# First layer's experts with tokens as rows, weighted after the multiplication

## The reference, cut to what matters

```python
gate_probs = softmax(xn @ gate_w.T + gate_b)          # 10 experts, 2 of them null
weights, selected = top_k(gate_probs, 2)              # null experts weigh nothing, the rest is normalised
combine_w = ...                                       # [tokens, 8], at most two entries of a row not zero
expert_out = einsum('td,edh->teh', xn, expert_w) + expert_b
ffn = einsum('te,teh->th', combine_w, expert_out)
x = x + attention(xn) + ffn
```

## Time and profile before

| what | value |
|---|---|
| time, median of three runs | 1821.56 us (1819.24 to 1825.79) |
| the profiled execution's own time | 1823.29 us |
| its span, first to last instruction | 1821.3 us |
| TensorE busy | 1721.1 us, 94% of the span |
| VectorE busy | 1015.6 us, 56% |
| ScalarE busy | 831.5 us, 46% |
| GpSimd busy | 385.6 us, 21% |
| mean granted TensorE clock | 0.958 |
| steps of `layer0_mix` | about 48 to 427 us of the span |

### The profile page before, as it was taken

How to read it: one execution, slowest core, us unless ns; L and a number is a source line. 1 busy time by engine, 2 the same in 40 slices (tenths; PEclk the granted TensorE clock), 3 DMA queues, 4 the chain that set the end, 5 groups by cost and what they waited for, 6 DMA issues and landing times. The chain is left out here.

```text
span 1821.3 us, 22776 instructions
## 1 busy us (share of the span) xinstructions
PE 1721.1 (94%) x8614; PEld 1009.8 (55%) x8614; DVE 1015.6 (56%) x1662; ACT 831.5 (46%) x1022; POOL 385.6 (21%) x306
## 2 busy tenths in 40 slices
PE   7899999998888998999999999999999997999996
PEld 4232222324443445787878787787878673444443
DVE  4555555544874444544544545555445447888885
ACT  4667777774333334343433433433434325434432
POOL 1000000000662002112120302011121204655552
PEclk8699999998868999999999999999999998999998
DMA  1222222223004540000000000000000010000001
GB/s 76 50 47 47 47 47 48 47 47 121 1 1 118 149 106 1 1 1 1 1 1 1 1 1 1 1 1 1 1 1 2 1 42 16 1 1 1 0 1 46
DMA packets 19128, 49.12 MB, mean 27 GB/s; under 512 B 784, under 2 KB 1680, under 8 KB 18128
## 3 DMA queue, kind: packets, MB, share of 16 engines
q1 hardware_dynamic: 19024, 47.70, 10.9%
HBM read 45.21 MB, written 2.36 MB: 26 GB/s over the span
## 5 line engine op out<-in xcount | busy, mean ns | idle before, releaser
L498 ACT ACTIVATE probs<-ps_ring 128x1024 f32<-128x1024 f32 x256 | 245.9, 1024 | 89.8 <-PE ps_ring L735 86.8
L1797 PEld LDWEIGHTS ps_o<-v,probs 128*128 128x128 f32 x2048 | 235.3, 192 | 31.0 <-issue 25.3
L1797 PE MATMUL ps_o<-v,probs 128*128 128x129 f32 x2048 | 248.1, 278 | 1.7 <-ACT probs L1522 1.2
L1522 ACT ACTIVATE probs<-ps_ring 128x1024 f32<-128x1024 f32 x128 | 127.0, 1024 | 212.2 <-PE ps_ring L1778 212.1
L1603 DVE TENSOR_REDUCE negmax<-ps_o 128x2 f32<-128x1024 f32 x64 | 78.5, 1226 | 137.2 <-PE ps_o L1753 137.2
L749 PE MATMUL ps_o<-probs,v 128*32 128x512 f32 x1024 | 139.9, 621 | 0.7 <-DVE o_sb L559 0.6
L1515 ACT ACTIVATE xn<-ps_ring,pack 128x512 f32<-128x512 f32 x64 | 40.5, 685 | 162.7 <-PE ps_ring L1362 162.7
L1977 POOL TENSOR_TENSOR rs<-r,state 128x512 f32<-128x512 f32 x64 | 86.1, 1347 | 115.0 <-DVE state L2124 114.8
L1616 DVE RECIPROCAL rden<-ps_o 128x2 f32<-128x2 f32 x128 | 21.5, 168 | 144.2 <-PE ps_o L1797 144.2
L735 PEld LDWEIGHTS ps_ring<-q_stack,k_stack 32*128 32x128 f32 x512 | 32.0, 186 | 123.9 <-issue 101.7
L2124 DVE TENSOR_TENSOR_SCAN state<-decay,state,kv 128x511 f32<-128x511 f32 x64 | 91.4, 1428 | 6.9 <-issue 1.6
(11 more groups left out here) (380 smaller groups left out, 3447.2 us busy)
## 6 DMA issues: line engine op xcount, KB each, us to landing
cwb<-combine_by_expert SPq DMA_DIRECT2D x8, 2048.0 KB
score<-score_by_expert SPq DMA_DIRECT2D x7, 2048.0 KB, 13.7
pack<-pack_dram SPq DMA_DIRECT2D x1, 3840.0 KB, 15.6
pack<-pack_dram SPq DMA_DIRECT2D x1, 2507.0 KB, 8.6
x<-x_in SPq DMA_DIRECT2D x2, 1024.0 KB, 6.4
out<-x SPq DMA_DIRECT2D x1, 2048.0 KB, 6.3
score<-score_by_expert SPq DMA_DIRECT2D x1, 1536.0 KB, 13.6
pack<-pack_dram SPq DMA_DIRECT2D x1, 1451.0 KB, 6.7
```

Source lines behind the costliest of these rows:

```text
L498: nc.scalar.activation(probs[n % 3][:, 2 * half:2 * half + 2, :], ps, ACT.Exp, scale=float(HD0) ** -0.5).then_inc(read, 1)
L1522: nc.scalar.activation(probs[:, n % 2, m, :, :], ps, ACT.Exp).then_inc(read, 1)
L1797: last = nc.tensor.matmul(ps_o[:, i, k * (D + 1):(k + 1) * (D + 1)], probs[:, (b * PAIRS + p) % 2, m, j, queries], v[:, m, h, :], start=(m ...
```

## The change

The rows and columns of the expert products are exchanged. For each block of 128 tokens, xn's high and low part are the stationary operand and the weights of four experts at a time the moving one (512 columns), so one use of the ring, `("ex", b, m)`, holds the outputs of all eight experts with tokens on the partitions. It takes six fp32r matmuls. VectorE's `mix` then reads the slot with one `tensor_scalar` and seven dependent `scalar_tensor_tensor` operations of 128 x 128, each scaled by the token's combine weight, a column of `cw`, with a drain before each of the seven; the last one frees the slot. TensorE turns the sum back with a product by the identity (`turn_mixed`) into `ps_y`. The experts come in steps 6, 8, 10 and 12, also in batch 0, the bias in step 12, the turns in steps 12 (two), 13 and 15. GpSimd splits xn of each batch, VectorE splits the expert weights once. `weigh`, the three `xe` buffers, the broadcast `cwb` and its eight loads of 2 MB are gone; `first`, which shared `cwb`'s memory, has its own.

```diff
+EXPERT_STEPS = (6, 8, 10, 12)
+TURN_STEPS = {12: (0, 1), 13: (2,), 15: (3,)}
...
+            if s in EXPERT_STEPS:
+                order.append(("ex", b, EXPERT_STEPS.index(s)))
...
                 if b:
-                    sp.wait_ge(xe_ready, b * E0_TRUE)
                     sp.wait_ge(biased, b)
-                here = sh["cw_dram"][:, at(b)]
-                sp.dma_start(cwb[:, :, :], here.unsqueeze(0).broadcast_to([P, E0_TRUE, T])).then_inc(cw_loaded, 16)
-                sp.dma_start(cwT[:, :], here).then_inc(cw_loaded, 16)
+                sp.dma_start(cwT[:, :], sh["cw_dram"][:, at(b)]).then_inc(cw_loaded, 16)
...
                 nc.gpsimd.tensor_tensor(sq[:, :, :], qk[:, :, :], qk[:, :, :], ALU.mult).then_inc(squared, 1)
+                if b > 1:
+                    was_read(pool, ("ex", b - 2, NBLK - 1))
+                nc.gpsimd.tensor_copy(single(xh[:, b % 2, :]), xn[:, at(b)])
+                pool.drain()
+                nc.gpsimd.tensor_tensor(single(xl[:, b % 2, :]), xn[:, at(b)], xh[:, b % 2, :], ALU.subtract).then_inc(x_split, 1)
...
+            def mix(b, m):
+                ps, read = filled(dve, ("ex", b, m))
+                if b:
+                    dve.wait_ge(mixed_turned, (b - 1) * NBLK + m + 1)
+                to, weight = mixed[:, m, :], cw[:, b * NBLK + m, :]
+                of = ps.rearrange("p a (e d) -> p (a e) d", d=D)
+                nc.vector.tensor_scalar(to, of[:, 0, :], weight[:, 0:1], None, ALU.mult)
+                for e in range(1, E0_TRUE):
+                    dve.drain()
+                    last = nc.vector.scalar_tensor_tensor(to, of[:, e, :], weight[:, e:e + 1], to, ALU.mult, ALU.add)
+                last.then_inc(read, 1)
+                dve.drain()
+                dve.sem_inc(mixed_ready, 1)
...
+            nc.vector.tensor_copy(single(expert_high[:, :]), w["expert0"])
             take_qk(0)
             take_v(0)
+            dve.drain()
+            nc.vector.tensor_tensor(single(expert_low[:, :]), w["expert0"], expert_high[:, :], ALU.subtract).then_inc(expert_split, 1)
...
                 copy_o(b, 0)
                 if follows:
                     take_v(b + 1)
+                if b == 0:
+                    store_rows()
+                    dve.drain()
+                mix(b, 0)
                 if b:
-                    weigh(b, 0)
-                    weigh(b, 1)
                     add(b - 1)
-                    weigh(b, 2)
...
+                mix(b, 1)
+                copy_o(b, 1)
+                mix(b, 2)
                 if follows:
                     scale_qk(b + 1)
...
+                mix(b, 3)
                 copy_o(b, 2)
...
-            def expert(b, e):
-                if e == 0 and b:
+            def experts(b, m):
+                ps, done = empty(pe, ("ex", b, m))
+                if m == 0:
+                    pe.wait_ge(x_split, b + 1)
+                    pe.wait_ge(expert_split, 1)
+                tokens = slice(m * P, (m + 1) * P)
+                for j in range(2):
+                    of = slice(j * T, (j + 1) * T)
+                    last = split_products(nc, ps[:, j, :], (xh[:, b % 2, tokens], xl[:, b % 2, tokens]),
+                                          (expert_high[:, of], expert_low[:, of]))
+                last.then_inc(done, 1)
+
+            def expert_bias(b):
+                if b:
                     pe.wait_ge(x_added, b)
-                n = b * E0_TRUE + e
-                pe.wait_ge(xe_ready, n + 1)
-                nc.tensor.matmul(ps_y[:, :], w["expert0"][:, e * P:(e + 1) * P], xe[:, n % 3, :],
-                                 start=(e == 0), stop=False).then_inc(xe_used, 1)
...
+            def turn_mixed(b, m):
+                pe.wait_ge(mixed_ready, b * NBLK + m + 1)
+                nc.tensor.matmul(ps_y[:, m * P:(m + 1) * P], mixed[:, m, :], sh["common"]["ident"], start=False, stop=False
+                                 ).then_inc(mixed_turned, 1)
...
-                    if b:
-                        if s >= 8:
-                            expert(b, s - 8)
-                    elif s >= 13:
-                        if s == 13:
-                            pe.wait_ge(cw_ready, 1)
-                        for e in ((0, 1), (2, 3, 4), (5, 6, 7))[s - 13]:
-                            expert(b, e)
-                    if s == 15:
+                    if s in EXPERT_STEPS:
+                        experts(b, EXPERT_STEPS.index(s))
+                    if s == 12:
                         expert_bias(b)
+                    for m in TURN_STEPS.get(s, ()):
+                        turn_mixed(b, m)
```

More of the change, by code:

```diff
@@ L384, in layer0_mix @@
         nd, rden, on = sb("nd", [P, 2, T]), sb("rden", [P, T]), sb("on", [P, T])
-        cwb = sb("cwb", [P, E0_TRUE, T])
         cwT = sb("cwT", [E0_TRUE, T])
-        xe = sb("xe", [P, 3, T])
+        xh, xl = sb("x0_high", [P, 2, T]), sb("x0_low", [P, 2, T])
+        expert_high, expert_low = sb("expert0_high", [P, E0_TRUE * P]), sb("expert0_low", [P, E0_TRUE * P])
+        mixed = sb("mixed0", [P, NBLK, D])
         lg, rank = sh["logits0"], sb("rank0", [P, NT, E0])
-        first = cwb[:, :, :].rearrange("p e t -> p (e t)")[:, 0:NT * E0 * E0].rearrange("p (t e f) -> p t e f", t=NT, e=E0)
+        first = sb("first0", [P, NT, E0, E0])
         stat, cw, cw_rows = sb("stat0", [P, 3 * NT]), sb("cw0", [P, NT, E0_TRUE]), sb("cw_rows0", [P, 2, P])
@@ L406, in layer0_mix @@
         o_copied, on_ready = sem("o_copied"), sem("on_ready")
-        xe_ready, xe_used = sem("xe_ready"), sem("xe_used")
+        expert_split, x_split = sem("expert0_split"), sem("x0_split")
+        mixed_ready, mixed_turned = sem("mixed_ready0"), sem("mixed_turned0")
         y_done, x_added = sem("y_done"), sem("x_added")
@@ L559, in copy_o @@
                 nc.vector.tensor_copy(o_sb[:, g, :], ps_o[:, :]).then_inc(o_copied, 1)
-            def weigh(b, e):
-                n = b * E0_TRUE + e
[L563 to L567, removed]
+            def mix(b, m):
[11 more added lines that the diff above has]
+                dve.sem_inc(mixed_ready, 1)
             def take_nd(b):
@@ L656, in _ @@
                     take_v(b + 1)
+                if b == 0:
+                    store_rows()
+                    dve.drain()
+                mix(b, 0)
                 if b:
-                    weigh(b, 0)
-                    weigh(b, 1)
                     add(b - 1)
-                    weigh(b, 2)
[L662 to L668, removed]
+                mix(b, 1)
+                copy_o(b, 1)
+                mix(b, 2)
                 if follows:
                     scale_qk(b + 1)
[L671 to L674, removed]
+                mix(b, 3)
                 copy_o(b, 2)
[L676 to L680, removed]
+                if follows:
                     take_rep(b + 1, 0)
-                if follows:
                     take_rep(b + 1, 1)
@@ L761, in place @@
                     last.then_inc(done, 1)
-            def expert(b, e):
-                if e == 0 and b:
-                    pe.wait_ge(x_added, b)
-                n = b * E0_TRUE + e
-                pe.wait_ge(xe_ready, n + 1)
-                nc.tensor.matmul(ps_y[:, :], w["expert0"][:, e * P:(e + 1) * P], xe[:, n % 3, :],
-                                 start=(e == 0), stop=False).then_inc(xe_used, 1)
-            def expert_bias(b):
-                pe.wait_ge(cw_loaded, b * 32 + 32)
-                nc.tensor.matmul(ps_y[:, :], w["expert0_b"][0:E0_TRUE, :], cwT[:, :], start=False, stop=False).then_inc(biased, 1)
+            def experts(b, m):
[11 more added lines that the diff above has]
+                if b:
+                    pe.wait_ge(x_added, b)
+                pe.wait_ge(cw_loaded, b * 16 + 16)
+                nc.tensor.matmul(ps_y[:, :], w["expert0_b"][0:E0_TRUE, :], cwT[:, :], start=True, stop=False).then_inc(biased, 1)
+            def turn_mixed(b, m):
+                pe.wait_ge(mixed_ready, b * NBLK + m + 1)
+                nc.tensor.matmul(ps_y[:, m * P:(m + 1) * P], mixed[:, m, :], sh["common"]["ident"], start=False, stop=False
+                                 ).then_inc(mixed_turned, 1)
             def output(b):
```

## The result

The changed kernel takes **1849.74 us** in the median (four runs, 1848.13 to 1853.8) where the kernel before takes 1822.53 (1819.24 to 1825.79): a ratio of 1.0145, 95% interval 1.0129 to 1.016. The profiled execution took 1848.13 us with a span of 1846.3, so the spans differ by 25.0 us.

A forecast was written before the change was run, and what follows sets the result against it. TensorE's own list was taken as the bound, lengthened by waits for slots held by `mix`: 1823.3 for the profiled execution, +17 for the layer, +14 for the clock, 1854; median 1853 us, range 1832 to 1880.

The forecast's parts named there:

- The mechanism: First layer: TensorE waits for ring slots that VectorE's `mix` holds, before the mean square and later scores.
- The slot's time: VectorE's `mix`: eight operations at 0.347 us plus seven drains, 3.3 us; a slot filled at t is empty at t + 3.75.
- rival 3: `mix` chain shorter, 0.258 us an operation: each wait shrinks by 0.7, 1818 us, no change; chance 0.05.
- The waits: TensorE idle 2.35 us before step 7's mean square, about 1.3 before scores of steps 10 and 12, 0.85 before 14.
- TensorE's saving: Each batch: 8.5 us of experts replaced by 5.5 of fp32r matmuls and 1.1 of turns, work falling 1.9 us.
- Batch 0: First batch of the first layer: without the late weights batch 1 starts at 99.0 instead of 104.50, so -5.5 us.
- The last two batches: Batch 6 at the usual +3.5 us; batch 7, with three waits of 1.3, at +1.6.
- The clock: Granted clock falls behind the wait before the mean square in most batches: 2.0 us for each of seven, +14.
- one of the signs that I had named against the forecast: Forecast is wrong if TensorE isn't idle before the mean square, the clock holds, or batches take under 45 us.
- rival 1: First layer's waits without the clock's fall: +17, about 1839 us; chance 0.22.
- Rival 4: No wait at all, TensorE's work governs: -1.9 x 8 and -5.5 for batch 0's loads, about 1802 us; chance 0.07.
- Costed at nothing: Splits of expert weights (0.69 and 1.23 us, VectorE) and xn (GpSimd), and SyncE's queue, taken as covered; weights uncovered: 2 us once.

The follow-up runs named there:

- four operations: Changed kernel with the outputs of experts 4 to 7 left out of VectorE's sum in `mix`: 1833.0 us, ratio 1.005 to the kernel before.
- one wide operation: Changed kernel, but `mix` multiplies the whole slot by broadcast combine weights into SBUF, then adds in three steps: 1830.2 us, ratio 1.0027 to the kernel before.
- The kernel without the late load: Kernel before, but batch 0's experts multiply by xn of batch 1 and don't wait for the 2 MB load: 1822.09 us, ratio 0.9996.
- three of seven in the next: The changed kernel run once more, unedited: 1853.31 us, ratio 1.0155 to the kernel before.
- The kernel with a single operation: Changed kernel with experts 1 to 7 left out of the sum in `mix`: 1829.17 us, ratio 1.0025 to the kernel before.
- the new placement: Experts in steps 8 to 11, two turns in step 13, two in next step 4; against wide product with sums on GpSimd: 1806.68 us, repeat 1806.91.
- spreading the experts: With the slot held: changed kernel's eight-operation `mix`, experts moved to steps 8 to 11: 1870.42 us, ratio 1.0261 to the kernel before.

## Why the prediction was right, and which of its terms were off

- *The mechanism* held. Eight experts for four ring slots read late, and the use three places behind waits: the mean square, and the scores of steps 10 and 12. The kernels with four operations and with one wide operation show it by its absence.
- *The slot's time*: I had 3.75 from a full slot to the held matmul; it is 3.49 (216.62 to 220.11). Each operation took 0.351 rather than 0.347 and the pitch of 0.43 was 0.42 (216.73 to 220.05 is 3.32 us for eight, as I had it). The latencies at both ends, 0.11 and 0.06, were smaller than the 0.3 I gave, and I had added 0.1 of reserve. By the formula that the Trainium skill, "VectorE: DVE Perf Modes", gives in its section on the TRN2 errata this operation would take 0.258 us, an estimate; 224 records here say 0.351, so the trace does not agree, and rival 3 is out.
- *The waits*: 2.35, 1.3, 1.3 and 0.85 were forecast, 1.99, 0.99, 0.82 and none measured, 3.8 us instead of 5.8. Before step 14 the profile shows none, because TensorE needed 6.87 us from step 12 to step 14 (235.63 to 242.50; 0.2 of them it waited for ScalarE) where I had 6.1 (the next point). The slot came free 6.8 us behind step 12, at 242.44, nearly when I had it (6.95): slot and list come out even there.
- *TensorE's saving*, 1.9 us, is the term that was mis-sized the other way. In a busy list an expert block costs 1.59 (215.03 to 216.62), not 1.4, since the first of a row of fp32r matmuls stands 0.34 from the second (225.04 and 225.38 in the block of step 8) and 0.1 follows the last; four of them are 0.8 dearer. The turns cost 0.64 for two, then 0.41 and 0.4, together 1.45 instead of 1.1. In the windows TensorE's idle time rose by 3.7 us a batch and its busy time fell by 0.3 only (43.45 to 43.11); of the 1.6 missing, the two prices explain 1.15, the rest I didn't find. The sum is near the +3.5 that I forecast, by errors of opposite sign: that this number came out is luck.
- *Batch 0* gained 3.5 us, with one fall of the clock in it, so about 5.0 without; forecast 5.5. The kernel without the late load shows that the load had cost 4.6. *The last two batches* cost 5.2; the forecast was 3.5 + 1.6. Without the two falls, at some 1.45 us each, the layer would be 17.4 us longer; forecast 17.
- *The clock* is the step that failed in size. I took 2.0 us in each of seven batches, 14 in all. It fell in two of seven in this trace and in three of seven in the next, 3.4 us long, for some 1.4 us each: 3 to 5 us. That it comes back soon, with dense work behind the wait, was right; that a wait of 2 us brings it down in most batches was not. That the clock holds was one of the signs that I had named against the forecast, and it held in five of seven. With it alone corrected the sum would be 1843, between my forecast and rival 1 (1839). The profiled execution has 4.6 us more behind the first layer, a term that my sum doesn't have and that no run explains; without it the median would be near 1845, and my forecast 8 us too high instead of 3. So the closeness of the total is luck too: 11 us too much for the clock, less 4.6 that I had nowhere.
- *Rival 4*, the faster case, had the wrong price. I let TensorE's sum of work govern, 1802, and named no other bound. The kernel with a single operation has no such wait and takes 1829. My count asked what TensorE does in a batch, not whether ScalarE keeps pace with it in each step; steps 6 and 12 are full, steps 9 and 11 empty, and ScalarE has its most work in 8 to 11. 1807 needs both the free slot and the new placement.
- *Costed at nothing*: the split of the expert weights took longer than I said, as the timeline of VectorE has it:

```profile
29.22 0.92 DVE L643 CAST expert_high<-pack 128x1024 fp32r<-128x1024 f32 x1
...
32.26 2.37 DVE L647 TENSOR_TENSOR expert_low<-pack,expert_high 128x1024 fp32r<-128x1024 f32 x1
```

  3.3 us for 1.9. It stayed covered: step 6 of batch 0 starts at 65.48, before at 66.53. GpSimd's split and SyncE's queue show up in no wait of TensorE.

Open is why the clock falls behind one wait of 1.99 us and not behind the next of the same length. In the two traces of the old form, too, nearly equal waits for the division in batch 7 ended differently: behind 1.07 us the clock held, behind 1.06 it fell. No run here separates what came before them.

## What to carry to other kernels

When a buffer goes round in a ring that an in-order engine fills, put the time for which a slot is held beside the work that stands between its filling and the use N places on, and let one wide operation free it before any chain of dependent ones. When work is moved between steps that two engines share, compare them step by step, and give the extra work to the steps in which the other engine is slow. A sum per batch shows neither, and a fix for one may harm until the other is made: here spreading the experts cost 20 us while the slot was held.

## What the runs showed of the hardware

VectorE and GpSimd can slow each other when both work on SBUF. In the kernel with the spread experts, GpSimd's sum of 512 columns takes 1.29 us beside VectorE's copy out of PSUM (1.28 where VectorE is idle) and 1.72 beside VectorE's scaling, and that scaling takes 2.43 instead of the 1.42 of the earlier trace rows; timelines of both engines:

```profile
211.23 1.29 POOL L459 TENSOR_TENSOR raw<-raw 128x512 f32<-128x512 f32 x1 [0.28 <-DVE raw L593]
...
217.28 1.72 POOL L459 TENSOR_TENSOR raw<-raw 128x512 f32<-128x512 f32 x1 [0.26 <-DVE raw L593]
```

```profile
211.07 0.68 DVE L584 COPY o_sb<-ps_o 128x512 f32<-128x512 f32 x1
...
217.12 2.43 DVE L567 SCALAR_TENSOR_TENSOR qk<-qk,pack,inv 128x512 f32<-128x512 f32 x2
219.64 1.05 DVE L570 CAST qk_high<-qk 128x1024 fp32r<-128x1024 f32 x1
```

The copy out of PSUM at 211.07 runs beside the same GpSimd sum and keeps its 0.68. The subtraction of the expert weights above, 2.37 instead of 1.23, also lay beside GpSimd's squaring and splitting (31.65 to 36.5); there the squaring kept its 1.89. The Trainium skill, "SBUF — State Buffer", section "Who interferes with whom", says that a VectorE instruction with two inputs in SBUF contends with a GpSimd one that reads SBUF, and that one with at most one such input outside the two-port modes doesn't. The trace agrees for the scaling, the subtraction and the copy. The cast has one input in SBUF and still took 1.05 instead of 0.69; in which mode it ran no run shows.

The other surprise is that code behind the changed layer took 2.4 to 6 us more in eight of ten traces of the new form (the table above), as much as some effects of this study. That is why the parts were read inside the first layer.
